# Six output banks, and the input's share of four outputs placed ahead of the last cell's share

## What is computed

```python
def step(c, xt):
    ft = sigmoid(xt @ wf.T + c @ uf.T + bf)
    it = sigmoid(xt @ wi.T + c @ ui.T + bi)
    gt = tanh(xt @ wc.T + c @ uc.T + bc)
    return ft * c + it * gt
c_final = scan(step, c0, x)
h = tanh(einsum('tbi,oi->tbo', x, wo) + c_final @ uo.T + bo)
```

## Time and profile before

| | |
|---|---|
| median of 3 runs | 2707.84 us (2706.66 to 2711.58) |
| the profiled execution | 2715.62 us |
| its span in the trace | 2713.8 us |
| PE busy | 2542.2 us (94%) |
| DVE busy | 2209.5 us (81%) |
| ACT busy | 1828.7 us (67%) |
| POOL busy | 1227.6 us (45%) |
| mean granted clock of PE | 0.97 |

### The profile page before, as it was taken

One profiled execution on the slowest core, in us unless ns is written; L12 is line 12 of the kernel. 1 busy time (PEld: TensorE's weight loads), 2 busy tenths in 40 slices (PEclk: granted clock), 3 DMA queues, 4 the chain that ended last, 5 costly groups with the idle time before them and its releaser, 6 DMA issues. The chain is left out here.

```text
span 2713.8 us, 34921 instructions
## 1 busy us (share of the span) xinstructions
PE 2542.2 (94%) x11075; PEld 1905.0 (70%) x11075; DVE 2209.5 (81%) x3128; ACT 1828.7 (67%) x3038; POOL 1227.6 (45%) x1258
## 2 busy tenths in 40 slices
PE   7899999996999999999999998899999999788888
PEld 4788888874666666666666665688888886467656
DVE  6687777777999999999999996787778875577665
ACT  4455555556888888888888885455555555566676
POOL 3566766664233233232332322466766663154411
PEclk9999999998999999999999999999999999788999
DMA  4566666644333333333333331566666650000000
GB/s 110 116 143 138 136 137 145 144 98 160 101 104 99 106 102 98 109 101 102 103 102 105 102 91 44 125 144 142 136 137 145 143 120 8 24 24 8 9 7 33
DMA packets 107384, 271.46 MB, mean 100 GB/s; under 512 B 30784, under 2 KB 35648, under 8 KB 107072
## 3 DMA queue, kind: packets, MB, share of 16 engines
q1 hardware_dynamic: 82192, 235.42, 35.4%
q0 software_dynamic: 24576, 33.62, 4.6%
q10 hardware_dynamic: 432, 0.20, 0.0%
HBM read 258.35 MB, written 10.76 MB: 99 GB/s over the span
## 5 line engine op out<-in xcount | busy, mean ns | idle before, releaser
L684 POOL TENSOR_TENSOR moe_experts_lo<-moe_experts_hidden,moe_experts_hi 128x512 fp32r<-128x512 f32 x512 | 662.4, 1294 | 340.5 <-ACT moe_experts_hi L622 340.3
L968 DVE TENSOR_TENSOR heads_e_lo<-heads_e,heads_e_hi 128x1024 fp32r<-128x1024 f32 x512 | 616.1, 1224 | 25.9
L629 ACT ACTIVATE psum<-psum 128x512 f32<-128x512 f32 x512 | 298.0, 582 | 478.6 <-PE psum L90 478.6
L802 POOL DMA_DIRECT2D heads_left<-heads_parts x512 | 307.5, 616 | 671.5 <-PE psum L856 610.3
L908 ACT ACTIVATE heads_e<-psum 128x1024 f32<-128x1024 f32 x512 | 520.8, 1024 | 108.0 <-PE psum L856 108.0
L656 DVE TENSOR_TENSOR moe_experts_weighted<-moe_spread,psum 128x512 f32<-128x512 f32 x512 | 351.3, 686 | 189.4 <-PE psum L90 185.7
L88 PE MATMUL psum<-heads_e_hi,heads_v_lo 128*128 128x512 f32 x1024 | 429.6, 420 | 18.3 <-DVE heads_u L934 18.3
L88 PE MATMUL psum<-moe_n_hi,moe_w_lo 128*128 128x512 f32 x1024 | 400.8, 391 | 5.6 <-PEq L54 5.4
L89 PE MATMUL psum<-heads_e_lo,heads_v_hi 128*128 128x512 f32 x1024 | 404.2, 395 | 0.0
L90 PE MATMUL psum<-heads_e_hi,heads_v_hi 128*128 128x512 f32 x1024 | 400.7, 391 | 0.0
L89 PE MATMUL psum<-moe_n_lo,moe_w_hi 128*128 128x512 f32 x1024 | 400.0, 391 | 0.0
(11 more groups left out here) (403 smaller groups left out, 4078.1 us busy)
## 6 DMA issues: line engine op xcount, KB each, us to landing
moe_spread<-moe_mask SPq DMA_DIRECT2D x128, 1024.0 KB, 10.2
heads_right<-heads_parts SPq DMA_DIRECT2D x512, 64.0 KB
heads_left<-heads_parts POOLq DMA_DIRECT2D x512, 64.0 KB, 2.5
heads_scale<-heads_inverse_copy SPq DMA_DIRECT2D x64, 512.0 KB, 3.7
moe_experts_raw<-in_gate SPq DMA_DIRECT2D x16, 256.0 KB, 11.7
moe_experts_raw<-in_up SPq DMA_DIRECT2D x16, 256.0 KB, 11.8
moe_experts_raw<-in_down SPq DMA_DIRECT2D x16, 256.0 KB, 11.7
heads_parts<-heads_e_hi SPq DMA_DIRECT2D x16, 256.0 KB, 3.2
```

The source lines that it names most:

```text
L629: act.activation(psum[:, GATE + p % 2, :], psum[:, GATE + p % 2, :], ACT.Silu).then_inc(silu_ready, 1)
L684: pool.tensor_tensor(lo[:, p, :], hidden[:, p % 2, :], f(hi[:, p, :]), ALU.subtract).then_inc(low_ready, 1)
L802: eng.dma_start(f(tile[row:row + 2 * HEAD, h % 2, :]), parts_dram[dims, order:order + 2, at]).then_inc(loaded[h % 2], 16)
L968: dve.tensor_tensor(e_lo[:, s, :], e[:, s % 4, :], f(e_hi[:, s, :]), ALU.subtract).then_inc(low, 1)
```

## The change

The outputs rotate over six banks, and before the last cell's share of the first output PE makes the input's share of outputs 0 to 3. From then on the input's share of output `n + 4` follows the last cell's share of output `n`. Four of the six banks also hold gate pieces, so PE waits there for the gate that read them.

```diff
-        OUT = 2
+        OUTS = (2, 3, 6, 7, 4, 5)
...
+                def output_from_input(n):
+
+                    at, bank = slice(n * BANK, (n + 1) * BANK), OUTS[n % len(OUTS)]
+                    for half in range(HALVES):
+                        if bank in SUMS[half]:
+                            pe.wait_ge(gates_ready, (BATCH - 1) * (3 * HALVES) + half * 3 + SUMS[half].index(bank) + 1)
+                    after(pe, h_ready, n - len(OUTS) + 1)
+                    product(pe, psum[:, bank, :], w["wo"], (n_hi[:, at], n_lo[:, at]), last=False)
+
+                AHEAD = 4
+                for n in range(AHEAD):
+                    output_from_input(n)
                 for n in range(BATCH * HALVES):
-                    half, bank, at = n % HALVES, OUT + n % 2, slice(n * BANK, (n + 1) * BANK)
-                    after(pe, h_ready, n - 1)
-                    product(pe, psum[:, bank, :], w["wo"], (n_hi[:, at], n_lo[:, at]), last=False)
+                    half = n % HALVES
                     if n < HALVES:
                         pe.wait_ge(low_ready, BATCH * HALVES + half + 1)
-                    product(pe, psum[:, bank, :], w["uo"], (c_hi[:, half, :], c_lo[:, half, :]),
+                    product(pe, psum[:, OUTS[n % len(OUTS)], :], w["uo"], (c_hi[:, half, :], c_lo[:, half, :]),
                             first=False).then_inc(out_ready, 1)
+                    if n + AHEAD < BATCH * HALVES:
+                        output_from_input(n + AHEAD)
...
-                    act.activation(h[:, n % 2, :], psum[:, OUT + n % 2, :], ACT.Tanh, bias=columns["bo"]).then_inc(h_ready, 1)
+                    act.activation(h[:, n % 2, :], psum[:, OUTS[n % len(OUTS)], :], ACT.Tanh, bias=columns["bo"]).then_inc(h_ready, 1)
```

## The result

The changed kernel takes 2698.1 us (median of 16 runs, 2695.39 to 2711.24) where the kernel before takes 2705.85 us (median of 16, 2702.18 to 2711.58). The ratio is 0.9976 with a 95% interval of 0.9967 to 0.9986: 6.5 us less, between 3.8 and 8.9. Forecast were 7.0 us less and 2700.8 us, with a range of 2698.3 to 2705.5; the median lies just outside its lower end, by 0.2 us. The kernel before was itself 2 us faster in this longer comparison than in the three runs that the forecast started from; 0.9976 of that base, 2707.84, would be 2701.3 us.

A forecast was written before the change was run, and what follows sets the result against it. PE was taken to bound the output part of both cells. Moved work 4.1 us plus clock 3.1, less 0.2 at the tail, gave 7.0 us off 2707.84, so 2700.8 us, range 2698.3 to 2705.5.

The forecast's parts named there:

- The fill: Before each cell's first `uo`: the moved `wo` matmuls fit into the wait; PE idle falls from 2.83 to about 0.8 us.
- PE's work behind the wait: First to last `uo` start: nine matmuls fewer save 2.04 us per cell, leaving 8.06 us at full clock.
- The clock: Both cells' outputs: clock stays up with 0.8 us idle, worth 1.5 and 1.6 us, 3.1 us for both.
- The new waits: Outputs 2 to 7: waits for gates or earlier tanhs are met when PE reaches them and cost nothing visible.
- ACT and DVE at the end: Outputs 4 to 7: ACT and DVE become the bound by a hair, 0.73 us per output, costing 0.1 us per cell.
- The stores: End of cell1: stores just fit, landing stays 2.0 us; taken as 0, up to 0.5 us if they queue.
- The sum: Both cells: 3.6 us in cell0 and 3.4 in cell1, together 7.0 us less.
- the clock falls all the same: Rival, cell outputs: 0.8 us idle still drops the clock; one cell -5.4 us, chance 0.09; both -3.9 us, 0.05.
- a stretch at half clock appears elsewhere: Rival, behind cell0: its earlier end brings a slow stretch, such as 2.5 us in cell1's beginning; total -4.5 us, chance 0.06.
- The two slower rivals: Clock swings under six-bank rotation in both cells' outputs, 2714.1 us, chance 0.02; decayed attention meets clock worse, 2714.8, 0.03.

The follow-up runs named there:

- spare work: Kernel before plus nine extra `wo` matmuls per cell, overwritten later, in the wait before the first `uo`; ratio 0.9994 (0.9984 to 1.0004).
- half change: The change in cell1 only, cell0 in the old order with six banks; ratio to the kernel before 0.9988 (0.9977 to 1.0000).
- the shares left out: Kernel before without the input's share of outputs 1 to 3, nothing put into the wait; ratio 0.9982 (0.9971 to 0.9993).
- six-bank run: The change with only output 0's input share ahead: six banks, matmul order of the kernel before; ratio to it 0.9994 (0.9983 to 1.0005).
- five ahead: The change with five outputs' input share ahead instead of four; ratio to the kernel before 0.9968 (0.9956 to 0.9980).

## Why the prediction came out as it did

*The fill* was right in every number: twelve matmuls from the end of the gate products, 0.79 us idle (0.8 forecast), the low part as late as before. *PE's work behind the wait*: 8.06 and 8.08 us for 8.06 forecast. The moved work is 2.04 us per cell, seen alone between the 10.11 us with spare work (45 matmuls at full clock) and the 8.06 of the change (36).

*The clock* was the open step. It stays up with 0.8 us idle: the change, the spare work and cell1 of the half change make five cells out of five at 1.00. The spare work shows the size without any other change, 1.5 and 1.6 us. That is what the two cells of the one profile before paid. Over all seven cells profiled with 2.83 us idle (two each of before, of six banks in the old order, and of the shares left out, one of the change in cell1 alone) the excess over full clock was 1.63, 1.49, 1.37, 1.61, 2.84, 1.70 and 2.90 us, on the mean 1.9 (13.00 - 10.1 = 2.90 in the last, 10.90 - 8.06 = 2.84 with 36 matmuls). By these cells the profile of the kernel before had the clock's price cheap, and the mean would make the term 3.9 us for both and not 3.1. Seven cells are few, and the whole times don't bear the larger term out: with it the sum would be 7.8 us where the ratio gives 6.5 (3.8 to 8.9), and the spare work alone gave 1.6 us with an upper end of 4.3. Which of 3.1 and 3.9 is nearer on the mean stays open.

*The new waits* cost nothing: no gap stands between the twelve `wo` matmuls, and the six-bank run has PE busy in full. The Trainium skill (TensorE: Matmul & The Clock Gate, "A second HAM failure mode: psum-queue depth-cycling") tells of a bf16 kernel whose 512-column matmuls, going round banks, paused between groups with the clock swinging. Here the outputs of the change ran busy in full at 1.00; with six banks in the old order PE was busy in full too, and the clock fell once per cell, behind the 2.83 us wait, as it does with two banks.

*ACT and DVE at the end* are the bound of the last four outputs in the change, as the step said, by little: 1.99 us from the last `uo` start to the last addition's end for 1.94 forecast (1.83 before). The working had one piece too small. It gave 1.46 us to a pair of outputs, with 0.05 from an addition's end to the tanh that waits for it; measured is 0.10, so a pair takes 0.68 + 0.83 = 1.51 us. In the last four outputs only one such wait comes, which makes the 0.05 us of difference; with five ahead two come, and that is the 0.1 us by which the 9.4 there was too good. *The stores*: 3.07 us from the last addition to the end of the span, 3.05 before. The DMA view gives:

```profile
out<-x SPq DMA_DIRECT2D x8, 256.0 KB, 2.1
```

for 2.0 in the earlier trace rows: they keep up.

*The sum*: the two cells gained 3.51 and 3.37 us in the profiles for 3.6 and 3.4 forecast. Whole runs say 6.5 us by the ratio and 7.75 by the medians, around 7.0. The forecast median was 2.7 us too high: 2 us of it is the base, 2707.84 from three runs against 2705.85 from sixteen.

*The rivals*: that the clock falls all the same was refuted in five cells, but with two outputs ahead, at 2.15 us of idle time, it came in three cells of four. That a stretch at half clock appears elsewhere did happen in the profile, in cell1's beginning (+1.64 us), while cell0's lost one (-2.82). It comes and goes with no change to the code: over all twelve profiles, with 3.19 us of idle time in front of the first gate product each time, cell0 took 36.4 us from there to its first `uo` seven times and 39.1 to 39.2 five times. cell1 took 36.4 twice and 38.0 ten times, and two of the ten are the six banks in the old order and the change in cell1 alone, where cell0 keeps the old order. So the +1.64 us needs no earlier end of cell0, and the profile of the kernel before was the lucky one there. Whether that earlier end shifts the clock on the mean was not settled; the half change bounds it to a few microseconds. The two slower rivals did not come: six banks in the old order kept their pace, and the decayed attention's mean clock was 0.84 where it was 0.82, on the good side. The whole stretch from cell0's last addition to cell1's first gate product took 328.0 to 336.9 us in the twelve profiles. The three whose cell0 does its work in the old order, with nothing added or left out, gave both ends of that (336.9, 332.9, 328.0), so the 4.26 us by which it is shorter in this pair of profiles need not come from the change either.

## What to carry to other kernels

Where an engine waits a few microseconds on others and then has work that hangs only partly on them, move the independent part into the wait, and count two gains: the work itself, and the clock that the matmul engine keeps. For the second it was enough here to shorten the idle time, even with useless work (seen in the stretch, not resolved over the whole time). Similar idle times elsewhere in the same trace, with their clock, give a first guess; a variant with the wait shortened by a different amount tests it. Read such a change in the stretch that it touches, and take the base of a forecast from many runs: here two profiles differed by 16.2 us, of which 6.9 were the change's.

## What the runs showed of the hardware

The granted clock after the idle time in front of the first `uo`, dense 512-column matmuls on both sides, by its length: 0.11 us, up in 4 cells of 4; 0.79 us, up in 5 cells of 5; 1.47 us, up in 4 of 4; 2.15 us, up in 1 of 4; 2.83 us, in 0 of 7. At 2.15 us the same program went either way. Where the clock fell behind 2.83 us, the price was 1.4 to 2.9 us. The 3.19 us in front of the cells' first gate products left the clock up in 9 of 24 cells, cell1 before and cell0 after among them, so the idle time's length alone does not decide. I had not expected the price itself to vary by a factor of two.

A handover between the two engines that work in turn: from the end of a tanh to DVE's start 0.03 us, from the end of an addition to the waiting tanh's start 0.10 us. With two buffers that is 1.51 us for two pieces of 128x512, with four buffers 1.36.
